# Layer-norm variances on GpSimd, half of z's scaling on ScalarE, and another order of the down products, in a kernel of a graph layer and a mixture of experts

## What is computed

```python
def gnn(x, adj_mx, alpha_train, w, d, fc_in_w, fc_in_b):
    h = einsum('bnd,ed->bne', x, fc_in_w) + fc_in_b
    alph = sigmoid(alpha_train)[:, None]
    w_eff = w * clip(d, 0, 1) @ w.T
    for _ in range(8):
        ax = einsum('nm,bmd->bnd', adj_mx, h)
        h = h + (1 / 8) * (alph * 0.5 * (ax - h) + h @ w_eff - h + x)
    return h

def moe(tokens):                      # 8 experts, the 2 best of each token
    probs = softmax(tokens @ router_w.T)
    combine = the two best of probs, divided by their sum, else 0
    out = tokens
    for e in range(8):
        out += combine[:, e:e+1] * (gelu(tokens @ w1[e] + b1[e]) @ w2[e] + b2[e])
    return out

x = x + gnn(layernorm(x), adj, ...)
x = x + moe(layernorm(x))
```

## Time and profile before

| | us |
|---|---|
| median of three runs | 551.6 (551.55 to 552.3) |
| the profiled execution | 552.14 |
| its span in the profile | 550.4 |
| granted TensorE clock | 1.00 |

### The profile page before, as it was taken

One profiled execution on the slowest core, in us unless ns is written; L12 is line 12 of the kernel. 1 busy time (PEld: TensorE's weight loads), 2 busy tenths in 40 slices (PEclk: granted clock), 3 DMA queues, 4 the chain that ended last, 5 costly groups with the idle time before them and its releaser, 6 DMA issues.

```text
span 550.4 us, 9148 instructions
## 1 busy us (share of the span) xinstructions
PE 532.5 (97%) x2895; PEld 459.4 (83%) x2895; DVE 445.4 (81%) x1140; ACT 303.3 (55%) x525; POOL 53.2 (10%) x42
## 2 busy tenths in 40 slices
PE   5999999999999999999999999999999999999796
PEld 4788997987799778987799778987799778998575
DVE  6988778689866996689867996699867995489995
ACT  5323433458535783458535783468535782148584
POOL 1102011101110101100110101100110101010100
PEclk9999999999999999999999999999999999999999
DMA  4030010292107601192107601292107501160151
GB/s 128 3 113 0 1 40 0 56 273 96 31 12 182 238 0 38 56 283 82 32 8 190 229 0 38 70 274 78 38 2 201 180 0 39 41 235 33 38 195 39
DMA packets 57374, 49.44 MB, mean 90 GB/s; under 512 B 26774, under 2 KB 51980, under 8 KB 55436
## 3 DMA queue, kind: packets, MB, share of 16 engines
q1 hardware_dynamic: 57356, 49.22, 29.5%
HBM read 41.61 MB, written 7.60 MB: 89 GB/s over the span
## 4 chain that ended last, share of the span: by engine, by line
issue 33%; PE 23%; DVE 22%; DMA 8%; ACT 5%; POOL 5%; SPq 3%; DVEq 0%; POOLq 0%
PE bank L1027 7%; PE bank L1029 7%; PE bank L1028 7%; DVE scs L578 7%; DVE work L892 5%; DMA x0q<-x_rows 4%; ACT x L406 3%; DMA x_rows<-x 3%; SPq L307 3%; POOL scr L377 3%; DVE scr L607 2%; DVE bn L582 2%; POOL rstd L368 2%; DVE Q L992 2%; ACT scs L398 1%
## 5 line engine op out<-in xcount | busy, mean ns | idle before, releaser
L398 ACT ACTIVATE scs<-work 128x512 fp32r<-128x512 f32 x132 | 83.3, 632 | 25.9 <-DVE work L892 25.9
L512 ACT ACTIVATE work<-bank,cols 128x512 f32<-128x512 f32 x128 | 86.9, 680 | 16.7 <-PE bank L1029 16.7
L578 DVE TENSOR_TENSOR scs<-work,scs 128x512 fp32r<-128x512 f32 x132 | 90.3, 685 | 2.0 <-ACT scs L398 0.5
L1027 PE MATMUL bank<-M,GT 128*128 128x384 f32 x192 | 64.3, 335 | 0.9 <-DVE GT L578 0.9
L1029 PE MATMUL bank<-M,GT 128*128 128x384 f32 x192 | 64.3, 335 | 0.0
L1028 PE MATMUL bank<-M,GT 128*128 128x384 f32 x192 | 64.2, 334 | 0.0
L892 DVE TENSOR_TENSOR work<-work,GT 128x512 f32<-128x512 f32 x90 | 60.7, 680 | 1.3 <-ACT work L512 1.1
L368 POOL TENSOR_TENSOR rstd<-ve,nhalf 128x8 f32<-128x8 f32 x16 | 30.5, 1909 | 292.1 <-DVE ve L598 292.1
L949 DVE TENSOR_TENSOR Q<-bank,bias 128x384 f32<-128x384 f32 x64 | 35.3, 552 | 25.0 <-PE bank L1029 24.0
L1027 PE MATMUL bank<-scs,w2s 128*128 128x512 f32 x128 | 53.0, 414 | 1.7 <-DVE scs L578 1.7
L398 ACT ACTIVATE GT<-bank 128x512 fp32r<-128x512 f32 x36 | 21.1, 595 | 60.4 <-PE bank L1029 57.9
(11 more groups left out here) (187 smaller groups left out, 1235.0 us busy)
## 6 DMA issues: line engine op xcount, KB each, us to landing
GT<-comb_rows SPq DMA_DIRECT2D x8, 1536.0 KB, 7.0
Q<-comb_rows SPq DMA_DIRECT2D x16, 512.0 KB, 7.1
GT<-comb_rows SPq DMA_DIRECT2D x7, 1024.0 KB, 5.7
xn<-in_x_dram SPq DMA_DIRECT2D x16, 256.0 KB, 7.9
out_dram<-outs SPq DMA_DIRECT2D x16, 256.0 KB, 2.3
GT<-comb_rows SPq DMA_DIRECT2D x7, 512.0 KB, 4.3
x_rows<-x SPq DMA_DIRECT2D x12, 256.0 KB, 2.6
x0q<-x_rows SPq DMA_DIRECT2D x24, 128.0 KB, 4.1
```

Source lines behind the costliest of these rows:

```text
L398: return nc.scalar.activation(dst, src, ACT.Copy)
L512: nc.scalar.activation(hid[:, i % 2, :], bank[UP_BANK[i % 3]][:, :], ACT.Gelu, bias=cols[:, B1_COL + e:B1_COL + e + 1]).then_inc(gelu_done, 1)
L578: return v.tensor_tensor(dst, src, hi.bitcast(FP32), ALU.subtract)
L1027: pe.matmul(dst, wh, xh, start=start, stop=False)
```

## The change

Five things are changed.

1. The variance chains of both norms leave VectorE. `ln_var` is gone; GpSimd does eight small operations in its place (`variance`), before the power, and now makes `shift` for both norms.
2. Of z, VectorE scales only batch 0 (behind items 4 and 5). ScalarE scales batch 1, one tile behind each of the high parts 4 to 7, in its items 5 to 8, with scale and shift as operands. Both wait for the second norm's shift.
3. A down product first takes its two matmuls with the item's high part (with the weights' high and low parts), which wait for that high part alone; the one with the item's low part comes last and waits for it.
4. The four tiles of node product 0 stand behind the down products 11 to 14, not behind the last one. The second follows the last down product, then the transpose of output 1, then the third.
5. Banks change places, so that node product 0 writes bank 0, free by then, while the down products add into bank 1.

```diff
-        GT_BANK = [2, 3, 0, 1]
-        Y1_BANK = [2, 3, 0, 1]
+        GT_BANK = [0, 3, 2, 1]
+        Y1_BANK = [0, 3, 2, 1]
...
+            def variance(n, g):
+
+                mean_e, mean_o = bn[:, n, :, 1], bn[:, n, :, 4]
+                pool.wait_ge(ln_own[n], T * g + T)
+                nc.gpsimd.tensor_tensor(mv[:, n, 1, :], mean_e, mean_o, ALU.subtract)
+                nc.gpsimd.tensor_tensor(mv[:, n, 2, :], bn[:, n, :, 2], bn[:, n, :, 5], ALU.add)
+                nc.gpsimd.tensor_tensor(mv[:, n, 0, :], mean_e, mean_o, ALU.add).then_inc(ln_sums[n], 1)
+                pool.wait_ge(ln_sums[n], 3 * g + 1)
+                nc.gpsimd.tensor_tensor(mv[:, n, 0, :], mv[:, n, 0, :], nhalf[:, :], ALU.mult)
+                nc.gpsimd.tensor_scalar(mv[:, n, 2, :], mv[:, n, 2, :], 1.0 / D, EPS, ALU.mult, ALU.add)
+                nc.gpsimd.tensor_scalar(ve[:, n, :], mv[:, n, 1, :], 0.25, None, ALU.mult).then_inc(ln_sums[n], 1)
+                pool.wait_ge(ln_sums[n], 3 * g + 2)
+                nc.gpsimd.tensor_tensor(mv[:, n, 1, :], mv[:, n, 1, :], ve[:, n, :], ALU.mult).then_inc(ln_sums[n], 1)
+                pool.wait_ge(ln_sums[n], 3 * g + 3)
+                nc.gpsimd.tensor_tensor(ve[:, n, :], mv[:, n, 1, :], mv[:, n, 2, :], ALU.add).then_inc(ln_ve[n], 1)
+
             def inverse_root(n, g):
+                variance(n, g)
                 pool.wait_ge(ln_ve[n], g + 1)
                 nc.gpsimd.tensor_tensor(rstd[:, n, :], ve[:, n, :], nhalf[:, :], ALU.pow).then_inc(ln_rstd[n], 1)
-                if n == 0:
-                    pool.wait_ge(ln_rstd[0], 2 * g + 1)
-                    nc.gpsimd.tensor_tensor(shift[:, :], mv[:, 0, 0, :], rstd[:, 0, :], ALU.mult).then_inc(ln_rstd[0], 1)
+                pool.wait_ge(ln_rstd[n], 2 * g + 1)
+                nc.gpsimd.tensor_tensor(shift[:, n, :], mv[:, n, 0, :], rstd[:, n, :], ALU.mult).then_inc(ln_rstd[n], 1)
...
+            def scale_z(g, b, t):
+                if t == 0:
+                    act.wait_ge(ln_rstd[1], 2 * g + 2)
+                k = GB * t + b
+                last = nc.scalar.activation(z[:, t, b, :], x1[:, t, b, :], ACT.Identity,
+                                            bias=shift[:, 1, k:k + 1], scale=rstd[:, 1, k:k + 1])
...
+                    if Z_SCALE < i <= Z_SCALE + NT and g is not None:
+                        scale_z(g, 1, i - Z_SCALE - 1)
...
-                    if i == 1 and g is not None:
-                        ln_var(1, g)
-                    if Z_SCALE <= i < Z_SCALE + 4 and g is not None:
-                        scale_z(g, (i - Z_SCALE) // 2, (i - Z_SCALE) % 2)
+                    if Z_SCALE <= i < Z_SCALE + 2 and g is not None:
+                        scale_z(g, 0, i - Z_SCALE)
...
-                        wait_low(pe, h, i)
-                        mm3(bank[SUM_BANK[b]][:, :], w2s[:, 0, e, :], w2s[:, 1, e, :],
-                            scs[:, i % RING, 0, :], scs[:, i % RING, 1, :], e == 0, e == E - 1).then_inc(down_mm, 1)
+                        pe.wait_ge(sc_hi, ITEMS * h + i + 1)
+                        for k in range(2):
+                            pe.matmul(bank[SUM_BANK[b]][:, :], w2s[:, k, e, :], scs[:, i % RING, 0, :],
+                                      start=(e == 0 and k == 0), stop=False)
...
+                        wait_low(pe, h, i)
+                        pe.matmul(bank[SUM_BANK[b]][:, :], w2s[:, 0, e, :], scs[:, i % RING, 1, :],
+                                  start=False, stop=(e == E - 1)).then_inc(down_mm, 1)
...
+                    if s >= ITEMS and more:
+                        if s == ITEMS:
+                            pe.wait_ge(x0_lo, GB * (g + 1) + GB)
+                        if s < ITEMS + NT:
+                            nodes_product_tile(0, s - ITEMS)
                 if more:
-                    pe.wait_ge(x0_lo, GB * (g + 1) + GB)
-                    pe.wait_ge(out_add, 1 + GB * h + 1)
-                    nodes_product(0)
+                    nodes_product(1)
                 transpose_out(h, 1)
                 if more:
-                    nodes_product(1)
+                    pe.wait_ge(out_add, 1 + GB * h + 1)
                     nodes_product(2)
```

More of the change, by code:

```diff
@@ L111, in build @@
         rstd = sb("rstd", [P, 2, T])
-        shift = sb("shift", [P, T])
+        shift = sb("shift", [P, 2, T])
         zT = sb("zT", [P, 2, GB, N], F32R)
@@ L406, in scale_x0 @@
                     last = nc.scalar.activation(x0[:, t // GB, t % GB, :], xn[:, t // GB, t % GB, :], ACT.Identity,
-                                                bias=shift[:, t:t + 1], scale=rstd[:, 0, t:t + 1])
+                                                bias=shift[:, 0, t:t + 1], scale=rstd[:, 0, t:t + 1])
                 last.then_inc(x0_ready, 1)
@@ L667, in _ @@
             dve.wait_ge(rows_t, 1)
-            v.tensor_copy(cols[:, 0:NT], bank[0][:, 0:NT]).then_inc(cols_ready, 1)
+            v.tensor_copy(cols[:, 0:NT], bank[2][:, 0:NT]).then_inc(cols_ready, 1)
             dve.wait_ge(sig_exp, 1)
@@ L953, in iteration @@
                         low_weights(i // 2)
-                    if not first and not final and i == 2:
-                        ln_var(0, g + 1)
                     if i == T - 3:
@@ L989, in iteration @@
                 dve.wait_ge(xq_ready, g + 1)
+                if not first:
+                    dve.wait_ge(ln_rstd[1], 2 * g)
                 for t in range(NT):
@@ L1069, in _ @@
             pe.wait_ge(alpha_in, 16)
[L1070 removed]
+            pe.transpose(bank[2][:, 0:NT], alpha_rows[:, :], ident[0:NT, 0:NT]).then_inc(rows_t, 1)
             for t in range(NT):
```

31 lines of the change are left out of this document (8 added, 23 removed).

## The result

| | before | after |
|---|---|---|
| median beside each other, us | 551.6 | 546.8 (545.3 to 548.7) |
| ratio, 95% interval | | 0.992 (0.990 to 0.994) |
| the profiled execution's span, us | 550.4 | 545.3 |

The changed kernel is faster by 4.8 us. The forecast had the direction, and its range (540.5 to 548.0) holds the time, but its sum said 8.9 us: a little over half of it came.

What follows compares the result with a forecast made beforehand. TensorE, busy 97% of the span, bounds the kernel, so only its holes can be gained: 3.7 + 1.2 + 1.2 + 1.6 + 1.2 = 8.9 us off 552.14 or the median 551.6, forecast 543.0 us, range 540.5 to 548.0.

Steps and rivals of the forecast that it cites:

- The forecast's own case: Whole kernel: the summed gains come and the time lies at 541 to 545 us; chance 0.62.
- Tail: Last down products of the experts: TensorE's wait for VectorE's low parts goes, 0.61 us x 6 = 3.7 us.
- Router product and down product 5: TensorE's wait for zT's second low part and the late down product of item 5 go: 0.2 x 6 = 1.2 us each.
- Up product 5: Item 5's up product waits for gelu 2; an earlier x0 reload shortens this, 2.8 - 1.2 = 1.6 us.
- GpSimd, "no cost": Second norm's chain on GpSimd: about 6.3 us, shift at 311.6, before the 312.0 from which TensorE loses; no cost.
- Final group: Last group, up to the combine weights: VectorE's saving shortens the end by 1.2 us, between 0.5 and 1.9.
- Setup: Chains before the loop: sooner start worth nothing, first up to 1.0 us later but swallowed by VectorE's waits; 0, at worst +1.
- What is late next: nothing that I find.: After the tiles move between the last down products, no new wait follows; VectorE's routing block starts about as much earlier.
- the signs that I had named: Profile after: right, no tail hole over 0.1, iterations 60.7 to 60.9 us; wrong, over 1 us waits for GpSimd's shift per iteration.
- half is given back: Experts blocks: GpSimd's chain or ScalarE's extra 1.6 us costs 0.3 to 0.8 each, or no earlier reload; 545 to 549; chance 0.20.
- The shift becomes the wait, slower: Second norm's chain: every GpSimd operation pays 0.67, shift at 313.8, time 558.0, or 551.7 at half the overshoot; chance 0.09.
- It doesn't do what it says: TensorE's holes only move, the tail's waits turning up at Q items 0 to 3; 550 to 552; chance 0.05.

Runs made afterwards that it cites:

- the interleave alone: Kernel before with only node product 0's tiles put between the last down products and the banks exchanged: 546.8 us, 548.1 in a second session.
- the chains alone: Kernel before with the variance on GpSimd and part of z's scaling on ScalarE, but the old down products, node products and banks: 546.6 us.
- the gelu 2 run: Changed kernel with ScalarE writing the high part of item 0 behind gelu 2 instead of ahead of it: 545.95 us.
- z one item later: Changed kernel with z's scaling one item later on both engines (VectorE behind items 5 and 6, ScalarE in items 6 to 9): 544.4 us.
- the four added operations: Changed kernel with four more small GpSimd operations, whose result nobody reads, in the second norm's chain: 557.2 us.

## Why the prediction was right and wrong

The forecast's own case, 541 to 545, did not come. The time lies in the range because the range took in most of a rival, which is the one that came. Step by step, sizes from the traces:

- **Tail, 3.7 us.** It goes fully, 0.61 in each iteration, and the interleave alone gives 3.5 to 3.8. The size is right. The credit is not: the chains alone empty the tail too. I had written that VectorE ends the experts up to 1.9 us earlier, and priced that at the router product and at down product 5, but not at the hole of 0.61 that stands behind both. Since the sum holds the tail once, it isn't wrong by this.
- **Router product and down product 5, 1.2 + 1.2.** Both gone: 0.3 to 0.08 per iteration at the first (0.08 also stays elsewhere, where a product follows transposes), 0.2 to nothing at the second. Right.
- **Up product 5, 1.6: the mis-sized term.** Over the six iterations this loss falls from 2.8 to 2.3 us, by 0.5. That the reload comes earlier was right. I had left 0.2 per iteration because the final group keeps that much, and overlooked what stands behind the reload: the chain over high part 0, as the gelu 2 run showed. It holds 0.27 + 0.11.
- **GpSimd, "no cost": the step that failed.** I had two numbers. The point from which the shift decides, 312.0 on that iteration's clock, is 8.2 us after up product 0; measured 8.0, so that was right. The shift's arrival, 311.6, is 7.8; measured 8.02 or 8.63. The chain began where I had put it (1.5 us after up product 0) and took 6.5 or 7.0 us where I took 6.3. I had some of its operations find VectorE idle; only the first one or two do, VectorE is never idle there once item 0 has begun, and six steps in a row pay 0.65. With 0.4 of room between two estimates, and each operation able to add 0.6 by which of two engines comes first, the honest entry was a chance of a cost, not zero. It cost 0.62 in two of six loop iterations of the first trace and in one of the second, and 0.63 in the final group of both.
- **Final group, 1.2: the second mis-sized term.** 0.2 measured. VectorE does 1.6 us less there from up product 0 to the combine weights, but stands 1.24 for the shift and 0.13 more later. I took 1.2 of the possible 1.9 while I charged no wait; the two don't go together, and z one item later, which removes the wait, brings 1.36 against before.
- **Setup, 0.** -0.3 in this pair of traces, but the traces scatter by more than 2 us here: not settled.
- **"What is late next: nothing that I find."** GpSimd's addition of x1 and z is moved onto VectorE's route by the interleave and holds it for 1.8 us in each iteration. I hadn't looked at it; the route had the room, so that the term is still zero.

Of the signs that I had named, the right ones came for the tail and in four of six iterations for the length (60.7 to 60.9 us). The wrong one came too: VectorE and ScalarE wait more than 1 us for the shift in the late groups (0.6 in the others), and up products of the range named wait for gelu. The combine weights didn't come 1 us sooner.

The terms as they came: 3.7 + 1.3 + 1.2 + 0.5 + 0.45 (a hole of 0.45 ahead of the second half of Y1, only in the first loop iteration, gone too) - 1.3 for the shift are 5.85, against 5.55 measured in the loop; 0.3 is not accounted for. With 0.21, -0.30 and -0.42 from the table above that makes the 5.0 between the profiled spans.

The rival that came about is **half is given back**, and by its first mechanism: both engines wait at the same shift. It had a chance of 0.20, and it should have had the larger one, given how near the two numbers stood. Its second mechanism, ScalarE's own 1.6 us, was not the cause; its third, no earlier reload, was wrong. **The shift becomes the wait, slower** named the right mechanism too, with 0.67 for every operation; the four added operations show what it would have been: 557. **It doesn't do what it says** fell: no hole has moved to the Q tiles.

The Trainium skill's rule that I quoted, "SBUF — State Buffer", section "Who interferes with whom", says that the two kinds of instruction exclude each other and that the second blocks until the first is done. The traces agree on both sides. In nearly every one of the small operations GpSimd pays (0.48 to 0.73 each in place of 0.20), while VectorE's own pitch stays 0.60 to 0.61 beside them. Beside GpSimd's addition of 2.4 us it is VectorE that pays: 2.05 in place of 0.22.

## What to carry to other kernels

Count how many parts of a change lean on the same hole: an engine that ends earlier fills every hole behind it, and parts that are each worth 3.7 and 5.7 us alone gave 5.6 to 6.0 together. Small operations moved to an idle engine cost their latency in a chain, here 0.65 us a step beside a working VectorE against 0.28 in quiet; find who asks for the end of the chain, and put the asking later before you shorten the chain (one constant gave 2 us here). And when two estimates lie closer together than the unit in which one of them jumps, book the jump with a chance, not as zero.

## What the hardware showed that I had not expected

**The clock after a wait.** In the last group TensorE waits 2.2 to 3.1 us for the combine weights, in every kernel here. In the profile of before the granted clock stayed 1.00 behind it, and in the second trace of the interleave too, with waits of 2.67 and 2.66. In the other twelve profiled executions it fell to half, the lower of the two levels (1.2 GHz), for a while. Stretches of after and, below, of the gelu 2 kernel:

```profile
515.50:520.00 4.50, 4.50 (x17) 3.65 (x18) 3.87 (x7) 2.79 (x5) 2.39 (x1) 0.62 0.32 87
...
513.60:519.80 6.20, 6.14 (x20) 5.28 (x21) 3.78 (x7) 3.21 (x7) 2.38 (x1) 0.50 0.51 120
```

Matmuls of 512 columns then start 0.42 to 0.43 apart instead of 0.23. The last group's experts took 25.30 us in the two traces without the fall and 25.49 to 26.98 with it, so it costs 0.2 to 1.7 us, and at nearly the same wait (2.73) both 0.2 and 1.7 were seen. The length of the wait does not decide alone; what does is not shown here. It is one source of the scatter between executions of one kernel, and the profile of before happened to be one without it, which makes the traces' difference 0.4 smaller than it would be.

**Two kinds of group.** The same code in the same loop lasts 60.78 or 61.40 us by whether one GpSimd operation of 0.2 us slips in ahead of a VectorE operation or has to wait for it. Which group it is changes from trace to trace: the first and third in one, the fourth in the other.
